# An adaLN transformer block in fp32: how tiles are split, what carries the shifts, and the orders of loads and TensorE

## What is computed

```python
mod = (silu(c) @ wmod).reshape(4, 6, 1, 512)          # sa, ca, ga, sb, cb, gb
ga, gb = (2 * (g >= 0) - 1) * maximum(abs(g), 0.25)   # for both gates
h = layernorm(x) * (1 + ca) + sa                      # x: (4, 512, 512)
qkv = h @ Wqkv + bqkv                                 # q, k, v: 128 wide, one head
x = x + ga * (softmax(q @ k.T / sqrt(128)) @ v @ Wo + bo)
h = layernorm(x) * (1 + cb) + sb
e = argmax(h @ gate_w.T + expert_bias)                # 4 experts, LoRA of rank 8
x = x + gb * (h @ W_up.T + lora_B[e] @ (lora_A[e] @ h))
```

## Time and profile before

| what | us |
|---|---|
| device time, median of 3 runs | 217.43 |
| lowest, highest | 215.95, 218.15 |
| span of the profiled execution | 216.5 |
| TensorE busy | 189.9 |
| VectorE busy | 155.9 |
| GpSimd busy | 119.5 |
| ScalarE busy | 113.8 |

### The profile page before, as it was taken

How to read it: one execution, slowest core, us unless ns; L and a number is a source line. 1 busy time by engine, 2 the same in 40 slices (tenths; PEclk the granted TensorE clock), 3 DMA queues, 4 the chain that set the end, 5 groups by cost and what they waited for, 6 DMA issues and landing times.

```text
span 216.5 us, 2939 instructions
## 1 busy us (share of the span) xinstructions
PE 189.9 (88%) x974; PEld 148.0 (68%) x974; DVE 155.9 (72%) x312; ACT 113.8 (53%) x210; POOL 119.5 (55%) x122
## 2 busy tenths in 40 slices
PE   7597799999879999499999999399999984998991
PEld 6437676776637787387888778288887853887870
DVE  0898796997989778974935949858343296899255
ACT  2813966669519885415677734247875421087110
POOL 1619172145978067943793929647938194662014
PEclk9969999999979999969999999979999997999999
DMA  5999849135000052000002060000210700202005
GB/s 166 343 375 261 288 173 362 53 100 191 4 0 0 3 195 97 2 0 3 2 32 113 3 132 13 0 2 0 75 73 0 145 0 3 94 4 97 3 0 194
DMA packets 13454, 19.49 MB, mean 90 GB/s; under 512 B 3920, under 2 KB 4432, under 8 KB 13440
## 3 DMA queue, kind: packets, MB, share of 16 engines
q1 hardware_dynamic: 13440, 19.31, 27.1%
HBM read 15.10 MB, written 4.21 MB: 89 GB/s over the span
## 4 chain that ended last, share of the span: by engine, by line
PE 54%; DVE 24%; POOL 9%; issue 5%; ACT 4%; DMA 2%; POOLq 0%; DVEq 0%; ACTq 0%
PE bank L384 34%; DVE xn L977 3%; POOL xs L1292 2%; POOL h2lo L1325 2%; PE bank L368 2%; PE bank L516 2%; PE bank L508 2%; PE bank L509 2%; PE bank L489 2%; PE bank L573 2%; DMA ga_bc<-gates_dram 2%; DVE alo L1040 1%; PE bank L423 1%; DVE xs L1061 1%; PE bank L462 1%
## 5 line engine op out<-in xcount | busy, mean ns | idle before, releaser
L1325 POOL TENSOR_TENSOR h2lo<-stage,h2hi 128x512 fp32r<-128x512 f32 x12 | 15.1, 1295 | 15.6 <-ACT h2hi L823 15.6
L1292 POOL TENSOR_TENSOR xs<-xs,gabo 128x512 f32<-128x512 f32 x16 | 21.8, 1384 | 0.2
L384 PE MATMUL bank<-alo,wqkv_hi 128*128 128x512 f32 x48 | 19.3, 402 | 1.8 <-DVE alo L1137 1.4
L384 PE MATMUL bank<-ahi,wqkv_lo 128*128 128x512 f32 x48 | 19.0, 395 | 0.0
L384 PE MATMUL bank<-ahi,wqkv_hi 128*128 128x512 f32 x48 | 18.9, 395 | 0.0
L738 ACT ACTIVATE xn_p<-xs,shift,rstd 128x512 f32<-128x512 f32 x16 | 12.7, 814 | 11.5 <-POOL shift L1304 11.3
L1333 POOL TENSOR_TENSOR xs<-xs,f_gb 128x512 f32<-128x512 f32 x12 | 15.4, 1299 | 5.6 <-DVE f_gb L1125 5.6
L1125 DVE TENSOR_TENSOR f_gb<-bank,gb_bc 128x512 f32<-128x512 f32 x12 | 8.0, 687 | 14.5 <-PE bank L573 7.8
L1318 POOL TENSOR_TENSOR alo<-stage,ahi 128x512 fp32r<-128x512 f32 x8 | 10.3, 1292 | 13.7 <-ACT ahi L731 13.7
L384 PE MATMUL bank<-wup_lo,h2hi 128*128 128x512 f32 x40 | 17.6, 440 | 0.0
L384 PE MATMUL bank<-wup_hi,h2hi 128*128 128x512 f32 x40 | 16.5, 414 | 0.0
(11 more groups left out here) (172 smaller groups left out, 556.5 us busy)
## 6 DMA issues: line engine op xcount, KB each, us to landing
out_dram<-xs SPq DMA_DIRECT2D x16, 256.0 KB, 2.1
xs<-in_L_attn_x_dram SPq DMA_DIRECT2D x3, 1024.0 KB, 5.5
stage<-in_L_wmod_dram SPq DMA_DIRECT2D x8, 256.0 KB, 5.0
xs<-in_L_wmod_dram SPq DMA_DIRECT2D x2, 1024.0 KB, 8.4
stage<-in_L_wmod_dram SPq DMA_DIRECT2D x2, 1024.0 KB, 11.5
xs<-in_L_attn_x_dram SPq DMA_DIRECT2D x4, 256.0 KB, 6.0
xs<-in_L_ffn_W_up_dram SPq DMA_DIRECT2D x1, 1024.0 KB, 8.3
ga_bc<-gates_dram SPq DMA_DIRECT2D x4, 256.0 KB, 4.1
```

Source lines behind the costliest of these rows:

```text
L384: mm = nc.tensor.matmul(dst, w, m, start=first and i == 0, stop=last and i == total - 1)
L1292: nc.gpsimd.tensor_tensor(xs[:, b, t, :], xs[:, b, t, :], gabo[:], ALU.add).then_inc(S["xb_ready"], 1)
L1325: nc.gpsimd.tensor_tensor(h2lo[:, kt, :], h2_full_at[b][:, kt, :], h2hi[:, kt, :].bitcast(F32), ALU.subtract).then_inc(S["h2_lo"], 1)
```

## The change

- Scale only in the split. h1 and h2 are no longer made as full tiles. ScalarE writes the high part as PSUM times (1 + ca), and VectorE makes the low part as PSUM times (1 + ca) minus high, for all batches. The shifts sa and sb go through the weights once: sa times Wqkv gives a bias of q, k and v for each batch (`qkv_shift_rows`, `qkv_shift_columns`, `qkv_shift`); sb times W_up gives rows of lbw, selected by constants in zst, and sb times the gate matrix a bias for gz (`ffn_shift`, `ffn_shift_rows`, `gate_shift`).
- The choice of the expert reads and writes PSUM, in the unused part of zl's bank; the two parts of gz are summed by a matmul with `fold`, so add_parts goes. The bank of zl is free only when zst is made.
- Own tiles for the splits of h1 (h1hi/h1lo) and p (phi/plo).
- Sections in the order ca, sa, ga, sb, cb, gb, all turned to columns; gates are worked on as columns and turned back (`gate_to_rows`).
- LayerNorm 1 of batches 1 to 3 is normalised by GpSimd.
- New orders of loads, of TensorE and the other engines, and a new plan of banks.

```diff
-    banks = {"mm": (0, 1, 2), "tp": (3, 4), "ff": (5, 6, 7)}
+        (6, "gateA"), (5, "loraB"),
+        (6, "mod", "sb"), (7, "qkv", 1, 0), (0, "qkv", 1, 1), (1, "qkv", 1, 2), (5, "modT", "sb"),
+    main, side = (7, 0, 1, 3, 4), (5, 6, 2)
...
+        steps += [("m", "zl", b - 1)] + [("m", "PT", b, t) for t in range(NT)] + [("s", "F", b - 1, 1)]
+        steps += [("m", "O", b), ("m", "zT", b - 1), ("s", "F", b - 1, 2)] + [("m", "Y", b, t) for t in range(NT)]
...
-                "gz": ("gz_ready", b + 1), "zl": ("z_step", Z_STEPS * b + 2), "zT": ("zT_ready", b + 1),
+                "gz": ("gz_ready", b + 1), "zl": ("zst_ready", 2 * b + 2), "zT": ("zT_ready", b + 1),
...
-            load_first("sa")
             load_first("ca")
             for t in range(NT):
                 sp.dma_start(xs[:, 0, t, :], x_v[0, :, t, :]).then_inc(x0_in[t], 16)
             for kt in range(NK):
                 sp.dma_start(raw["wqkv"][:, kt, 0:3 * D], wqkv[kt * P:(kt + 1) * P, :]).then_inc(wqkv_in[kt], 16)
+            load_first("sa")
...
+                for t in range(NT):
+                    mm = nc.tensor.matmul(dst[:, t * GZ:(t + 1) * GZ], gz[:, t * P:(t + 1) * P], fold[:],
+                                          start=True, stop=True)
...
-                    nc.scalar.activation(h1_full_at[b][:, kt, :], at("x1T", b, kt)[:], ACT.Identity,
-                                         bias=modT["sa"][:, kt, b:b + 1], scale=modT["ca"][:, kt, b:b + 1]
-                                         ).then_inc(S["h1_full"], 1)
-                    nc.scalar.activation(ahi[:, kt, :], h1_full_at[b][:, kt, :], ACT.Copy).then_inc(S["h1_hi"], 1)
+                    nc.scalar.activation(h1hi[:, kt, :], at("x1T", b, kt)[:], ACT.Copy,
+                                         scale=modT["ca"][:, kt, b:b + 1]).then_inc(S["h1_hi"], 1)
...
-                    nc.vector.tensor_tensor(alo[:, kt, :], h1_full_at[b][:, kt, :], ahi[:, kt, :].bitcast(F32),
-                                            ALU.subtract).then_inc(S["h1_lo"], 1)
+                    nc.vector.scalar_tensor_tensor(h1lo[:, kt, :], at("x1T", b, kt)[:], modT["ca"][:, kt, b:b + 1],
+                                                   h1hi[:, kt, :].bitcast(F32), ALU.mult,
+                                                   ALU.subtract).then_inc(S["h1_lo"], 1)
...
+            def ln1_normalise(b):
+                pool.wait_ge(S["ln1_rstd"], NT + b)
+                pool.wait_ge(S["x1T_psum"], NK * b)
+                for t in range(NT):
+                    nc.gpsimd.tensor_scalar(xn1[:, t, :], xs[:, b, t, :], moments[:, 0, t, 0:1], rstd[:, 0, t:t + 1],
+                                            ALU.subtract, ALU.mult).then_inc(S["xn1_ready"], 1)
...
+                zl = at("zl", b)[:, 0:NT * GZ].rearrange("p (t g) -> p t g", t=NT)
+                equal = at("zl", b)[:, EQ_AT:EQ_AT + NT * E].rearrange("p (t e) -> p t e", t=NT)
+                nc.vector.tensor_tensor(first, equal, first_wins[:], ALU.mult).then_inc(S["z_step"], 1)
```

More of the change, by code:

```diff
@@ L113, in psum_plan @@
+    place, earlier, holds = {}, {}, [None] * 8
+    for bank, *name in order:
         place[tuple(name)] = bank
@@ L373, in open_bank @@
                 if before is not None:
-                    ready, count = last_read(*before)
+                    ready, count = emptied(*before)
                     pe.wait_ge(S[ready], count)
@@ new lines, in last_x2_transposes @@
+            def last_x2_transposes():
+                b = LAST
+                for t in range(NT):
+                    pe.wait_ge(S["xn2_ready"], NT * b + t + 1)
+                    for kt in range(NK):
+                        dst = open_bank("x2T", b, kt) if t == 0 else at("x2T", b, kt)
+                        mm = nc.tensor.transpose(dst[:, t * P:(t + 1) * P], xn2_p[:, t, kt * P:(kt + 1) * P], ident[:])
+                        if t == NT - 1:
+                            mm.then_inc(S["x2T_psum"], 1)
@@ new lines, in _ @@
+            for b in range(1, B):
+                last = b == LAST
+                scores(b)
+                v_transposes(b)
+                if last:
+                    up(b - 1, 0)
+                else:
+                    up(b - 1, 0, (0, 1))
+                    x1_transposes(b + 1)
+                    up(b - 1, 0, (2, 3))
+                z_to_tokens(b - 1)
+                p_transposes(b)
+                up(b - 1, 1)
+                pv(b)
+                z_transposes(b - 1)
+                up(b - 1, 2, (0, 1))
+                out_projection(b)
+                lora_up(b - 1, 0)
+                lora_up(b - 1, 1)
+                up(b - 1, 2, (2, 3))
+                lora_up(b - 1, 2)
+                up(b - 1, 3)
+                lora_up(b - 1, 3)
+                if not last:
+                    qkv(b + 1, (0, 1))
+                    x2_transposes(b)
+                    qkv(b + 1, (2, 3))
+                    gate_and_lora_a(b)
@@ new lines, in _ @@
+            wup_high((2, 3))
+            h2_high(0)
+            gate_rows_evacuate("gb")
+            qkv_evacuate(1)
+            act.wait_ge(S["fb_psum"], 1)
+            nc.scalar.activation(fb_hi[ZROWS:P, :].bitcast(F32R), at("fb")[ZROWS:P, :], ACT.Copy).then_inc(S["fb_hi_ready"], 1)
+            gz_evacuate(0)
+            for b in range(1, B):
+                last = b == LAST
+                softmax(b, (0, 1, 2))
+                v_evacuate(b)
+                softmax(b, (3,))
+                if not last:
+                    h1_high(b + 1)
+                pt_high(b)
+                o_high(b)
+                zT_evacuate(b - 1)
@@ new lines, in _ @@
+            split_sb()
+            inverse_sums(0)
+            mod_low("cb", (1,))
+            o_low(0)
+            mod_low("cb", (3,))
+            residual(0, 0)
+            ln2_moments(0, 0)
+            residual(0, 1)
+            ln2_moments(0, 1)
+            residual(0, 2)
+            ln2_moments(0, 2)
+            residual(0, 3)
+            ln2_moments(0, 3)
+            wup_low((0, 1))
+            scale_columns("cb")
+            mod_low("gb", (1, 3))
+            wup_low((2, 3))
@@ L1221, in _ @@
+            gate_columns("gb")
+            ln1_stats(2, (0, 1, 2, 3))
+            ln1_moments(2)
+            h2_low(0)
+            qk_low(1)
+            ffn_shift_rows()
+            gate_shift()
+            for b in range(1, B):
+                last = b == LAST
+                maxima(b)
+                v_low(b)
+                if not last:
+                    h1_low(b + 1)
+                pt_low(b)
+                choose_expert(b - 1)
+                inverse_sums(b)
                 if b + 2 < B:
@@ L1383, in _ @@
+            for b in range(1, B):
+                last = b == LAST
+                add_output_bias(b)
+                if not last:
+                    output_weights(b + 1)
+                ln2_deviation(b, (0, 1))
+                outputs(b - 1, (0,))
+                ln2_deviation(b, (2,))
+                outputs(b - 1, (1,))
+                ln2_deviation(b, (3,))
+                if not last:
+                    split_output_weights(b + 1)
+                outputs(b - 1, (2, 3))
                 if b + 2 < B:
```

1243 lines of the change are left out of this document (588 added, 655 removed).

## The result

The changed kernel takes 226.87 us (median of 4 runs, 226.16 to 227.31) where the kernel before takes 217.53 beside it: a ratio of 1.043, with a 95% interval of 1.0385 to 1.0476. The forecast was 222.9 within 211 to 230, slower. The direction and the range hold; the point is 4 us low. The profiled execution has a span of 224.6, and took 226.62.

The account below looks back on a forecast made before the run. TensorE, busy 88% of the span, and its waits were taken as the bound. Stages 18.9 + 17.2 + 25.6 + 28.4 + 80.2 + 51.7 gave 222.0 us, plus 0.9 made 222.9; range 211 to 230.

Parts of the forecast that it names:

- A: Stage from the start to the first matmul of the first projection: 23.8 us before, 18.9 forecast (17.9 to 20.5).
- B: Stage from the first projection to the first scores matmul: 11.2 us before, 17.2 forecast (16.1 to 18.1).
- E: Two batches, from batch 1's scores to batch 3's: 84.35 us before, 80.2 forecast (77.5 to 84.4).
- F: The end, from the scores of batch 3: 56.75 us before, 51.7 forecast (49.5 to 54.5).
- C: Stage from the first scores to the first output projection: 20.4 us before, 25.6 forecast (23.2 to 27.5).
- D: Stage from the first output projection to batch 1's scores: 20.0 us before, 28.4 forecast (25.5 to 31).
- 0.9: Added to the forecast span of 222.0 us because the earlier runs' median, 217.43, lay 0.9 above the span.
- tensor_scalar on GpSimd (12 of 512 columns) is in no row: Unknown price of GpSimd's normalisations: taken as 1.3 us each; 1.73 was said to move nothing, 0.65 to gain nothing.
- The gate is no bound.: In the stage up to the first output projection: gate needed 7.1 us before; here 18 us are there.
- The first: Rival, faster: prologue queues run freely, TensorE's clock doesn't fall, batch 1's scores before 84.6; time 210.6 us, chance 0.22.
- The second: Rival, no change: gb's low halves come early enough before batch 1's scores, that stage 23, time 217.5 us; chance 0.14.
- The third, the slow choice: Rival: expert's choice stays slow beside GpSimd, p times v pays 4.05 us more three times, time 235; chance 0.08.

Follow-up runs that it names:

- The first experiment: Changed kernel with GpSimd's two low halves of section sb moved behind batch 1's four normalisations; 224.1 us, ratio 1.0331 to the kernel before.
- the second experiment: Changed kernel with ScalarE's and VectorE's split of gzw moved ahead of the splits of p; 222.71 us, ratio 1.0285 to the kernel before.
- the three orders together: Changed kernel with sb's low halves behind the normalisations, gzw's split ahead of p's, gb's low halves ahead of output_weights(1); 222.41 us, ratio 1.0263.
- The pair of kernels with GpSimd busy: Changed kernel with four more GpSimd products beside the choice: its tiles in PSUM 226.67 us (ratio 1.045), in SBUF 238.63 us (1.1001).

## Why the prediction came out as it did

- **The method.** Cut by stages, the walk gave 222.0 for a span of 224.6. Five of six stages were within 1.5 us, and the errors of A, B, E and F (-3.2) hid part of those of C and D (+5.8). That the sum came as close as it did is thus in part luck. The time also lies 2.3 above the span, where I had added 0.9. So the 4.0 by which the point was low is 2.6 of walk and 1.4 of that offset. The 0.9 was too small because it set the median of the runs against the span of the slowest of them: that execution took 218.15, 1.65 above its own span of 216.5.
- **A, 18.9 against 18.3.** Right: loads of x ahead of section sa, and one section less on VectorE before the statistics. VectorE's first statistics start at 9.01, where I had 9.3. It was read from the traces, not tried by itself.
- **B, 17.2 against 15.7.** The order of the wait was right, its size not (1.11, not 2.9). VectorE's walk was priced at the upper rows: sa's sum and split took 0.5 where 0.8 stood, and sb's two low halves 1.28, the lower of the two rows. No experiment touched this stage, and its loss is left in every kernel here.
- **C, 25.6 against 30.0.** Here the step failed that begins "tensor_scalar on GpSimd (12 of 512 columns) is in no row": 2.08 a tile, above both bounds (0.65 and 1.73), and "1.73 moves nothing, since the next user is 5 us away" was wrong besides: from 35.05 on, four tiles of 1.73 end at 42.0, 1.2 after TensorE is free at 40.8, and only at 1.3 each would they have been in time (40.3). I had counted the distance to the user, but not what stands ahead in GpSimd's queue: the deviation at 31.20 and two low halves of sb until 35.05. Four tiles from there end at 43.4, and x1T(1) started 9.4 after the scores, not 7.0. Behind the wait of 2.65 the transposes of x1T(1) took 3.50, not 1.97, another 1.5; the granted clock there was 0.54. All six profiles with that wait have 3.4 to 3.7 for them, and of the seven without it six have 1.97 and one 3.51 (last section). The first experiment took both away and C was 26.0, next to the 25.6 of the walk. Section sb's wait was right to 0.3, and the second experiment shows its cause.
- **"The gate is no bound."** True in the changed kernel, where its spread is used at 46.26. True only while the queue ahead of it is clear: the three orders together made it the bound.
- **D, 28.4 against 29.85.** The mechanism and its place were right; I had GpSimd's two low halves of gb at 1.3 each and they took 1.7 beside VectorE's, as this row of GpSimd's timeline in the changed kernel shows, with the two products that stand ahead of them ending at 75.78.

```profile
75.74 3.39 POOL L1305 TENSOR_TENSOR h2lo<-xs,h2hi 128x512 fp32r<-128x512 f32 x2
```

- **E, 80.2 against 79.6.** Right: p times v waits for zst, 1.16 where I said 1.7, and no choice is over 3 us. The gain against before is only in part the choice's. Of the waits in the earlier trace rows the 3.4 lies in E, the 4.2 in F. The other wait that E had before, in batch 1, the prediction does not name: p's low halves stood behind VectorE's four normalisations, which are GpSimd's now.

```profile
85.38 5.69 DVE L977 TENSOR_SCALAR xn<-xs,moments,rstd 128x512 f32<-128x512 f32 x4 [0.62 <-POOL rstd L1259]
```

```profile
91.72 0.47 PE L554 MATMUL bank<-ident,gz 72*128 72x72 f32 x4 [3.01 <-DVE alo L1040]
```

So 3.0 and 3.4 became 1.16 twice, 4.1 of the 4.8 gained. The pair of kernels with GpSimd busy shows a mechanism that makes waits for the choice. The kernel before was not run with its choice in PSUM, so for its own waits that cause is argued from the earlier trace rows.
- **F, 51.7 against 51.2.** The last matmul came 46.9 after the scores, as said; the terms within were not tried one by one.
- **The rivals.** The first (210.6, all stages at their low bounds) fell by its own point: batch 1's scores at 93.8, not before 84.6. The second fell with D. The third, the slow choice, fell, and for the reason given.
